# Newton-Schulz on X and its transpose: a second product in place of a turn, and a X inside the polynomial

## The reference

```
X = G / (sqrt(sum(G * G)) + 1e-7)          # G: 64 x 64, for 3 weights x 4 heads
for a, b, c in NS_COEFFS:                  # 5 sets of coefficients
    A = X @ X.T
    B = b * A + c * (A @ A)
    X = a * X + B @ X
```

## Time and profile before

| what | value |
|---|---|
| median of 3 runs (lowest to highest) | 861.67 us (861.62 to 861.74) |
| span of the profiled execution | 860.0 us, 27595 instructions |
| what lies around the span, against the median | 1.67 us |
| busy: PE, PEld | 811.3 us (94%), 700.2 us (81%) |
| busy: DVE, ACT, POOL | 715.6 (83%), 369.5 (43%), 406.7 us (47%) |
| transposes of X at line 701 | 450 matmuls, 64.2 us busy |
| each of the three kinds of small product | 1800 matmuls, 68.6 to 72.7 us busy |

### The profile page before, as it was taken

The page is one execution under the profiler, slowest core; times in us unless marked ns, Lnnn a source line. Parts: engine busy times, 40 slices in busy tenths (PEclk is TensorE's granted clock), DMA queues, the critical chain, the costliest instruction groups (busy, mean ns, idle before and its releaser), DMA issues.

```text
span 860.0 us, 27595 instructions
## 1 busy us (share of the span) xinstructions
PE 811.3 (94%) x9926; PEld 700.2 (81%) x9926; DVE 715.6 (83%) x2592; ACT 369.5 (43%) x868; POOL 406.7 (47%) x535
## 2 busy tenths in 40 slices
PE   3899999999999999999999999999999999999997
PEld 2888888888888788888888888888888888888886
DVE  4789798897988979889798897988979889798876
ACT  2444344443444434444444444444444444444433
POOL 1644545445454454544545445544455444544442
PEclk9899999999999999999999999999999999999999
DMA  8100000000000000000000000000000000000000
GB/s 326 35 3 14 8 2 19 0 12 6 0 18 0 12 6 0 18 0 12 6 0 18 0 12 6 0 18 0 12 6 0 18 0 12 6 0 12 0 12 7
DMA packets 9716, 13.77 MB, mean 16 GB/s; under 512 B 1120, under 2 KB 8928, under 8 KB 9440
## 3 DMA queue, kind: packets, MB, share of 16 engines
q1 hardware_dynamic: 7904, 7.80, 3.1%
q10 hardware_dynamic: 1792, 5.70, 1.7%
HBM read 11.41 MB, written 2.10 MB: 16 GB/s over the span
## 4 chain that ended last, share of the span: by engine, by line
PE 62%; DVE 26%; issue 7%; ACT 2%; POOL 1%; DMA 1%; DVEq 1%; SPq 0%; ACTq 0%
PE CB L630 13%; PE M L630 13%; PE YB L630 11%; PE HB L630 9%; PE CA L630 7%; DVE acc L1322 5%; PE CA L701 5%; DVE Wn L1169 4%; DVE X L1140 2%; DVE dhb L1089 2%; POOL r L286 1%; DVE Am L1126 1%; DVE Mp L1132 1%; DMA rows<-in_rows 1%; DVE r L1233 1%
## 5 line engine op out<-in xcount | busy, mean ns | idle before, releaser
L364 POOL TENSOR_TENSOR hq<-hr 128x512 f32<-128x512 f32 x128 | 136.3, 1065 | 77.7 <-ACT hr L427 76.2
L286 POOL TENSOR_TENSOR r<-r,half 128x3 f32<-128x3 f32 (+1 forms) x78 | 77.9, 1011 | 157.6 <-DVE r L1111 68.6
L630 PE MATMUL HB<-xlT,e_s 128*128 128x128 f32 x1024 | 144.0, 284 | 0.4 <-ACT xlT L427 0.4
L630 PE MATMUL YB<-e_s,hq 128*128 128x128 f32 x1024 | 141.6, 281 | 0.8 <-DVE acc L1322 0.8
L342 POOL TENSOR_TENSOR aX<-X,a_tile 128x192 f32<-128x192 f32 x150 | 92.9, 639 | 88.9 <-DVE X L1140 88.9
L630 PEld LDWEIGHTS HB<-xlT,e_s 128*128 128x128 f32 x1024 | 126.9, 193 | 7.7 <-ACT xlT L427 0.7
L427 ACT ACTIVATE hr<-HB 128x512 f32<-128x512 f32 x128 | 76.4, 597 | 130.0 <-PE HB L630 129.9
L1322 DVE SCALAR_TENSOR_TENSOR acc<-YB,cw,acc 128x128 f32<-128x128 f32 x448 | 125.5, 343 | 7.6 <-PE YB L630 7.6
L630 PEld LDWEIGHTS YB<-e_s,hq 128*128 128x128 f32 x1024 | 124.2, 192 | 5.6 <-issue 1.3
L427 ACT ACTIVATE XT<-CA 64x384 f32<-64x384 f32 x150 | 65.7, 477 | 63.3 <-PE CA L701 63.2
L630 PEld LDWEIGHTS CA<-Am 64*64 64x64 f32 x1800 | 60.8, 134 | 21.3 <-issue 15.9
(11 more groups left out here) (178 smaller groups left out, 1458.5 us busy)
## 6 DMA issues: line engine op xcount, KB each, us to landing
xa<-in_x SPq DMA_DIRECT2D x16, 128.0 KB, 2.0
e_s<-in_e1T ACTq DMA_DIRECT2D x1, 2048.0 KB, 12.7
e_s<-in_e2T ACTq DMA_DIRECT2D x1, 2048.0 KB, 19.0
xr<-in_x SPq DMA_DIRECT2D x16, 128.0 KB, 2.1
out<-ot SPq DMA_DIRECT2D x16, 128.0 KB, 1.7
wall<-in_wall SPq DMA_DIRECT2D x1, 820.0 KB, 6.8
up_s<-in_upT ACTq DMA_DIRECT2D x1, 512.0 KB, 14.1
down_s<-in_downT ACTq DMA_DIRECT2D x1, 512.0 KB, 19.6
```

The costliest lines, as they stand in the source:

```text
L286: return pool.tensor_tensor(dst, src, expo[:, 0:n], ALU.pow)
L364: pool.tensor_tensor(hq[b][:, :, :], hr[b][:, :, :], hr[b][:, :, :], ALU.mult).then_inc(e_hq, 1)
L630: return pe.matmul(out_, lhsT, rhs, start=start, stop=stop)
```

## The change

The transpose of X is no longer turned after each iteration. A second set of six products makes X_new^T = X^T Mp, where Mp now holds the term a X: A becomes A + (a/b) I before it enters the polynomial, so that c Mp X is the whole new X. GpSimd makes the shifted A (`AmI`) after VectorE's copy of A, in place of `aX` after X. Stage 3 of an iteration issues, for each group, the products for the transpose into `CA` and then those for X into `CB` (only the latter in the last iteration). ScalarE's copy of the transpose takes c as its scale and is now 128 partitions x 192 elements; the first iteration still turns X and copies it in two halves. The gram product goes into `CA`, and the square into `CB`.

```diff
-            def ax(i, g, it):
-                pool.wait_ge(e_x[g], (NI + 1) * i + it + 1)
-                pool.tensor_tensor(aX[g], X[g], a_tile[:, it, :], ALU.mult).then_inc(e_ax[g], 1)
+            def a_shift(i, g, it):
+                pool.wait_ge(e_am[g], NI * i + it + 1)
+                pool.tensor_tensor(AmI[g], Am[g], shift[:, it], ALU.add).then_inc(e_shifted[g], 1)
...
-                    if st % 4 == 0:
+                    if st % 4 == 1:
                         for g in range(G):
-                            ax(i, g, st // 4)
+                            a_shift(i, g, st // 4)
...
             def xt(i, g, it):
                 act.wait_ge(e_t[g], NI * i + it + 1)
-                a(XT[g], CA[g][0:HD, 0:3 * P], ACT.Copy).then_inc(e_xt[g], 1)
+                if it == 0:
+                    for h in range(2):
+                        c = slice(h * HD, (h + 1) * HD)
+                        ins = a(XT[g][c, :, :], CA[g][0:HD, 0:3 * P].rearrange("p (w c) -> p w c", w=3)[:, :, c], ACT.Copy)
+                    ins.then_inc(e_xt[g], 1)
+                else:
+                    a(XT[g], CA[g][:, 0:3 * HD], ACT.Copy, scale=NS[it - 1][2]).then_inc(e_xt[g], 1)
...
+            def ns_square(g, it):
+                am_in[g].wait()
+                if it > 0:
+                    x_in[g].wait(skip=1 if it == NI - 1 else 0)
+                ns_pair(g, CB, Am, Am).then_inc(e_prod[g], 1)
+
+            def ns_apply(g, it):
+                mp_in[g].wait()
+                if it < NI - 1:
+                    ns_pair(g, CA, X, Mp).then_inc(e_t[g], 1)
+                ns_pair(g, CB, Mp, X).then_inc(e_prod[g], 1)
...
             def ns_m(i, g, it):
                 dve.wait_ge(e_prod[g], 3 * NI * i + 3 * it + 2)
-                scalar_tensor_tensor(Mp[g], Am[g], b / c, CA[g], ALU.mult, ALU.add).then_inc(e_mp[g], 1)
+                dve.wait_ge(e_shifted[g], NI * i + it + 1)
+                scalar_tensor_tensor(Mp[g], AmI[g], b / c, CB[g], ALU.mult, ALU.add).then_inc(e_mp[g], 1)
             def ns_x(i, g, it):
                 dve.wait_ge(e_prod[g], 3 * NI * i + 3 * it + 3)
-                dve.wait_ge(e_ax[g], NI * i + it + 1)
-                scalar_tensor_tensor(X[g], CB[g], NS[it][2], aX[g], ALU.mult, ALU.add).then_inc(e_x[g], 1)
+                tensor_scalar(X[g], CB[g], NS[it][2], None, ALU.mult).then_inc(e_x[g], 1)
...
-            for it in range(NI):
-                nc.vector.memset(a_tile[:, it, :], NS[it][0])
...
+            dve.wait_ge(e_ident, 16)
+            tensor_tensor(eye, ident[:, 0:HD], ident[:, HD:P], ALU.add).then_inc(e_eye, 1)
+            dve.wait_ge(e_eye, 1)
+            for it in range(NI):
+                tensor_scalar(shift[:, it], eye (broadcast over w), NS[it][0] / NS[it][1], None, ALU.mult)
```

More of the change, by code:

```diff
@@ L105, in build @@
         neghalf = sb("neghalf", [P, 8])
-        a_tile = sb("a_tile", [P, NI, 3 * HD])
+        eye = sb("eye", [P, HD])
+        shift = sb("shift", [P, NI, 3, HD])
         bdones, mask, mask_prev = fixed[:, 0, :], fixed[:, 1:3, :], fixed[:, 3, :]
@@ L118, in build @@
         X = [sb(f"X{g}", [P, 3, HD]) for g in range(G)]
-        aX = [sb(f"aX{g}", [P, 3, HD]) for g in range(G)]
-        XT = [sb(f"XT{g}", [HD, 3, P]) for g in range(G)]
+        AmI = [sb(f"AmI{g}", [P, 3, HD]) for g in range(G)]
+        XT = [sb(f"XT{g}", [P, 3, HD]) for g in range(G)]
         Am = [sb(f"Am{g}", [P, 3, HD]) for g in range(G)]
@@ L222, in build @@
         e_dw, e_G, e_s3, e_ssb, e_sst, e_pw, e_x = (per_group(n) for n in ("dw", "G", "s3", "ssb", "sst", "pw", "X"))
-        e_ax, e_t, e_xt, e_am = (per_group(n) for n in ("aX", "turn", "XT", "Am"))
+        e_shifted, e_t, e_xt, e_am = (per_group(n) for n in ("AmI", "turn", "XT", "Am"))
         e_prod, e_mp = (per_group(n) for n in ("product", "Mp"))
@@ L229, in build @@
         e_ap, e_prT, e_av, e_at2, e_comb, e_ct, e_combT = (sem(n) for n in ("probs_turned", "prT", "att_pv", "att_steps", "comb", "comb_turned", "combT"))
-        e_mask = sem("mask_ready")
+        e_mask, e_eye = sem("mask_ready"), sem("eye")
         e_rt, e_cw = sem("route_steps"), sem("cw_ready")
@@ L338, in ss_pow @@
                 power(r3[g][:, 2, :], r3[g][:, 1, :], half, 3).then_inc(e_pw[g], 1)
-            def ax(i, g, it):
-                pool.wait_ge(e_x[g], (NI + 1) * i + it + 1)
-                pool.tensor_tensor(aX[g][:, :, :].rearrange("p w c -> p (w c)"),
-                                   X[g][:, :, :].rearrange("p w c -> p (w c)"), a_tile[:, it, :],
-                                   ALU.mult).then_inc(e_ax[g], 1)
+            def a_shift(i, g, it):
+                pool.wait_ge(e_am[g], NI * i + it + 1)
+                pool.tensor_tensor(AmI[g][:, :, :].rearrange("p w c -> p (w c)"),
+                                   Am[g][:, :, :].rearrange("p w c -> p (w c)"),
+                                   shift[:, it].rearrange("p w c -> p (w c)"), ALU.add).then_inc(e_shifted[g], 1)
             def row_pow(m, g):
@@ L478, in xt @@
                 act.wait_ge(e_t[g], NI * i + it + 1)
-                a(XT[g][:, :, :].rearrange("p w c -> p (w c)"), CA[g][0:HD, 0:3 * P], ACT.Copy).then_inc(e_xt[g], 1)
+                if it == 0:
[4 more added lines that the diff above has]
+                else:
+                    a(XT[g][:, :, :].rearrange("p w c -> p (w c)"), CA[g][:, 0:3 * HD], ACT.Copy, scale=NS[it - 1][2])\
+                        .then_inc(e_xt[g], 1)
             def w_T(m, g):
@@ L618, in _ @@
         def _(pe):
-            x_turn = [Expect(pe, e_x[g], f"x_turn{g}") for g in range(G)]
+            x_in = [Expect(pe, e_x[g], f"x_in{g}") for g in range(G)]
             xt_in = [Expect(pe, e_xt[g], f"xt_in{g}") for g in range(G)]
@@ L696, in sums, with ns_turn @@
                 mm(CB[g][:, 0:3], bdones[:, :], r3[g][:, 0, :]).then_inc(e_ssb[g], 1)
-            def ns_turn(g, last_step):
-                x_turn[g].wait(skip=1 if last_step else 0)
+            def ns_turn(g):
+                x_in[g].wait()
                 for w in range(3):
@@ L702, in ns_turn, with ns_pair @@
                 ins.then_inc(e_t[g], 1)
[L704 to L714, removed]
+            def ns_pair(g, bank_, left, right):
                 for w in range(3):
@@ L718, in ns_pair, with ns_gram @@
                         ins = mm(bank_[g][c, w * HD:(w + 1) * HD], left[g][c, w, :], right[g][c, w, :])
-                ins.then_inc(e_prod[g], 1)
+                return ins
+            def ns_gram(g):
+                xt_in[g].wait()
+                ns_pair(g, CA, XT, XT).then_inc(e_prod[g], 1)
+            def ns_square(g, it):
[8 more added lines that the diff above has]
+                ns_pair(g, CB, Mp, X).then_inc(e_prod[g], 1)
             def turn_w(m, g):
@@ L917, in body @@
                         if st % 4 == 0:
-                            ns_turn(g, st // 4 == NI - 1)
+                            if st == 0:
+                                ns_turn(g)
                             if st == 0 and g == 0:
@@ L925, in body @@
                         elif st % 4 == 2:
-                            ns_pair(g, CA, am_in, Am, Am)
+                            ns_square(g, st // 4)
                         else:
-                            ns_pair(g, CB, mp_in, Mp, X)
+                            ns_apply(g, st // 4)
                     for f in fill.get(st, []):
@@ L1125, in ns_a @@
                 dve.wait_ge(e_prod[g], 3 * NI * i + 3 * it + 1)
-                nc.vector.tensor_copy(Am[g][:, :, :].rearrange("p w c -> p (w c)"), CB[g][:, 0:3 * HD]).then_inc(e_am[g], 1)
+                nc.vector.tensor_copy(Am[g][:, :, :].rearrange("p w c -> p (w c)"), CA[g][:, 0:3 * HD]).then_inc(e_am[g], 1)
             def ns_m(i, g, it):
@@ L1138, in ns_x @@
                 dve.wait_ge(e_prod[g], 3 * NI * i + 3 * it + 3)
-                dve.wait_ge(e_ax[g], NI * i + it + 1)
-                nc.vector.scalar_tensor_tensor(X[g][:, :, :].rearrange("p w c -> p (w c)"), CB[g][:, 0:3 * HD], NS[it][2],
-                                               aX[g][:, :, :].rearrange("p w c -> p (w c)"), ALU.mult, ALU.add)\
-                    .then_inc(e_x[g], 1)
+                nc.vector.tensor_scalar(X[g][:, :, :].rearrange("p w c -> p (w c)"), CB[g][:, 0:3 * HD], NS[it][2], None,
+                                        ALU.mult).then_inc(e_x[g], 1)
             def row_sums(m):
@@ L1389, in _ @@
             ln_norm(0)
+            dve.wait_ge(e_ident, 16)
+            nc.vector.tensor_tensor(eye[:, :], ident[:, 0:HD], ident[:, HD:P], ALU.add).then_inc(e_eye, 1)
+            dve.wait_ge(e_eye, 1)
+            for it in range(NI):
+                nc.vector.tensor_scalar(shift[:, it], eye[:, :].unsqueeze(1).to_broadcast([P, 3, HD]),
+                                        NS[it][0] / NS[it][1], None, ALU.mult)
             dve.wait_ge(e_ttw, 16 * G)
```

2 lines of the change are left out of this document (1 added, 1 removed).

## The result

| kernel | median us (lowest to highest, runs) | against the kernel before, 95% interval |
|---|---|---|
| before | 861.7 (861.62 to 862.52, 4) | |
| changed | 895.02 (894.17 to 895.43, 4) | 1.0387 (1.0372 to 1.0401), slower |

The changed kernel's profiled execution has a span of 893.6 us and took 895.43. Over 15 tiles the 33.3 us are 2.2 us a tile. The prediction was 895.5 us. Two of its terms were far off, in opposite directions, so the agreement of the total is in part luck; the experiments show the true parts.

What follows compares the result with a forecast made beforehand. The prediction took a full TensorE queue to bound the Newton-Schulz phase, with one link on VectorE. It summed 1.6 + 0.65 = 2.25 us a tile, x 15 = 33.8 us, to 895.5 us (range 889 to 901).

Steps and rivals of the forecast that it cites:

- What bounds the kernel: Newton-Schulz phase is a full TensorE queue, not a latency chain; one link, X to Mp in iterations 2 to 3, is VectorE's.
- Part 1, TensorE's queue: Iterations 0 to 3: 24 added matmuls at 0.84 us replace turns at 0.65; net 0.76 us a tile, 11.4 us.
- lower bound of part 3: Up to Mp of iteration 3: 0.9 us, since X of the second group waits for all 48 products even without n8.
- Part 2, the copies: ScalarE's late XT copies stall TensorE 0.2 us at stage 7 to 8 and 0.5 us at stage 15 to 16.
- Part 3, the shift: Stage 9: n8 queues behind GpSimd's shifts, VectorE waits; Mp of iteration 3 is 1.55 to 1.6 us later.
- The walk: Before-and-after times at stage 9: ss8 ends 431.55 instead of 430.52, n8 434.8 instead of 432.23, qkn 435.95 instead of 434.30.
- Part 4, the last iteration: Stage 17: gram late by 0.5 us, the shifts add 0.15 before Mp; 0.65 us, bounds 0.4 and 1.1.
- Mp released by GpSimd at stage 17: Sign expected in the changed profile: at stage 17 Mp is released by GpSimd.
- TensorE's sum alone: Rival: VectorE's and GpSimd's lateness is swallowed by waits; 11.4 us or less plus one copy stall, 873 us, chance 0.14.
- More lock: Rival: the shifts also hold up routing steps and the token normalisation, +0.6 us a tile, 905 us; chance 0.12.
- n8 does no harm: Rival: 0.9 us up to Mp of iteration 3 plus the end's 0.65, 1.55 x 15 = 23, 885 us; chance 0.22.
- The faster rival: The chain decides, not the queue: 0.48 us a tile gained, 854.5 us, if TensorE's idle time exceeds 0.76 us; chance 0.04.

Runs made afterwards that it cites:

- e11: e3 with the products for the transpose left out too (TensorE's 1440 added matmuls gone): 832.9 us, ratio 0.9653.
- e3: Changed kernel without the shifted A, and XT copies moved ahead of h_relu(5) (for stage 8) and the table load (for stage 16): 866.41 us, ratio 1.0048.
- e2: Changed kernel without GpSimd's shifted A; Mp made from A itself, the term a X left out: 879.84 us, ratio 1.021.
- e5: Complete changed kernel with XT copies ahead of h_relu(5) (for stage 8) and the table load (for stage 16): 883.99 us, ratio 1.0243.
- e9: Complete changed kernel with one wait added on GpSimd: h_sq(5) starts only when VectorE has finished qkn: 879.32 us, ratio 1.0194.
- e4: Changed kernel with the power in prep_n8 replaced by a multiplication, nothing moved: 880.11 us, ratio 1.0198.
- e6: Changed kernel with GpSimd's power n8 ahead of the two shifts of stage 9 instead of behind them: 894.35 us, ratio 1.0369.
- e1: Kernel before with the shifted A in place of aX, the turns of X kept: 880.34 us, ratio 1.0213.

## Why the prediction came out, point by point

**What bounds the kernel: right.** Until iteration 2 the tile is a full TensorE queue: e11 loses 0.7 us for each stage of 24 products taken away, and in e3 VectorE's ss8 stands at +0.04.

**Part 1, TensorE's queue: sized wrong.** The step "24 matmuls ... cost what a like stage costs, 0.84 us" took the price of a stage with its start-up. In the earlier trace rows the 0.84 hold about 0.14 for leaving the wide shape (0.49 for the first 12 against 0.35 for the others); products added to a stage that is already running don't pay that again. They cost 0.70, and the turn 0.65. For the first swap the net is the 0.05 that this gives, by the starts of TensorE's gram products in the tile (11.78 and 11.82 us in iteration 0 for the kernel before and e3, 19.27 and 19.35 in iteration 1). The second costs 0.23 (26.85 and 27.16), for a reason that no run looks into, and the third 0.05 again (33.89 and 34.25). That makes 0.33, while three iterations came to 0.57 in my sum. My lower bound, 0.78, was too high as well. The first 12 against the next could be read in the old chain, had I split it by group. About 0.25 us a tile do follow from the products in another way, which the prediction had only as a lower bound of part 3: X comes behind 48 of them, and VectorE waits.

**Part 2, the copies: right at stage 15 to 16, another path at 7 to 8.** Stage 15 to 16: 0.5 predicted, 0.56 in the waits. Stage 7 to 8: a stall of TensorE of 0.2 predicted, and there is none; its gram products start at 27.16 us of the tile with the late copies and with the early ones (e3). The late copy works through VectorE instead: ss8 is 0.48 late, of which 0.08 were there before, and Am of both groups stands behind it. With both places, 0.9 us a tile (e2 less e3, 13.4 us, the hold of qkn in e2 among them) against 0.7. With the shift in place they are worth 11.0 us (e5). The table load took 1.28 us with the copy 0.02 behind it, as before, so the drain of the Trainium skill's page (ScalarE: Activation LUTs, What ACT_TABLE_LOAD costs) isn't seen here either: what the load costs is its place in the list.

**Part 3, the shift: place right, mechanism half right, sized wrong.** Two errors ran against each other. The walk had the step behind n8 about 1.6 us late (434.8 against 433.18); it is 0.92 late (31.58 against 30.66 us of the tile). Most of the difference is that of ss8, 1.03 late in the walk and 0.48 in the trace: 48 products take 1.54 us and not 1.68, and ScalarE's steps, which I had added end to end to 1.47 us from HB's end to the second copy, overlap and take 1.18 (444.27 to 445.45). Against it, the prediction took the chain behind n8 as 1.12 us, as before, and it came to 2.52 (449.80 to 451.07 + 1.25). h_sq(5) had run ahead of these steps (432.19 to 433.23 us before), and h_sq(6) behind them and `aX`; now both run right when the steps do and take the port twice. The wait for n8 itself is worth little, at most 0.14 at the second X (e9). e4 and e6 can't say this: in e4 qkn is held without the wait, and in e6 another wait takes its place. The Trainium skill (SBUF — State Buffer, Who interferes with whom) has it that, of a GpSimd and a VectorE operation that both need the shared port pair, the later one blocks until the other is done, and the rows bear it out: `gs`, with two SBUF inputs, ends at 436.81 and GpSimd's square at 436.79, and the tensor_scalar of eight elements ends at 450.80 and its square at 450.77. I had named the rule for stages 5 and 17 and for `gs`, and not for the very steps whose delay I was computing. I even credited the squares' earlier slot at `gs` with 0.25 us; it gives 0.5 (e1: +1.88 to +1.31).

**Part 4, the last iteration: the first half right, the second nil.** The gram's 0.5 us is there; the extra 0.15 us of the shift at stage 17 isn't: e2 and e4, without and with the shift, are at +1.21 and +1.22 at the second Mp of iteration 4. Mp released by GpSimd at stage 17 was one of the signs that I had named, and it isn't in the trace: VectorE's waits there are for TensorE.

**The sum.** Predicted: 1.6 up to Mp of iteration 3 and 0.65 behind it. Measured: 1.76 and 0.53 (at the second Mp of iteration 4), less 0.1 in the tail. But the 1.6 were composed of 0.57 for products, 0.2 for the copy and 0.8 for n8; as differences of runs at that Mp they are about 0.25 for products (e3), 0.4 for the copy (e2 less e3) and 1.1 for the port (the changed kernel less e9). The overcharge of the products, the step behind n8 put too late, and the missing hold of the port cancelled, and that is luck.

**The rivals.** TensorE's sum alone, at 873, is refuted in its size (e3: 866) and as the cause. "More lock" had the kind of cause right and the steps wrong: the lock costs 1.1 us a tile, at r and qkn, while the token normalisation takes 1084 ns against 1085 before. Other terms were smaller than forecast, so the total isn't 905. "n8 does no harm" is what e4 shows, but by 880 and not 885. The faster rival needed more than 0.76 us of idle time; the net charge turned out as 0.05 to 0.23 an iteration, so it was nearer than its chance said: with every order repaired the changed kernel is still 0.56% (0.40 to 0.71) slower.

**Left open.** The 0.3 us a tile that e3 keeps are seen on VectorE's wait for X; making the products for X before those for the transpose would test this. It wasn't run. Why the second swap costs TensorE 0.23 us and the others 0.05 is open too.

## What to carry to other kernels

When engines work through lists written by hand, the price of an edit is mostly in who stands behind the moved instruction: here 27 of 33 us were places in ScalarE's and GpSimd's lists and went away without touching the arithmetic. When a wait is taken off or delayed on VectorE, look also at what GpSimd will be doing at the new time, since a tiny step can be held for a whole GpSimd operation; a wait added on the engine that is ahead can be a gain. And price work added to a running stage by its second group, not by a stage that pays the start.

## What I had not expected of the hardware

- One added wait on GpSimd made the kernel 15.7 us faster (e9). The square had started 0.07 us before an 8-element step of VectorE, which then took 1.00 us instead of 0.16.
- Small products cost 0.35 us for 12 behind other small products and 0.49 behind wide ones. The 0.35 holds with one bank written for each group (a stage of 24 in 0.84) and with two (48 in 1.54).
- The gram product with its two halves on different partitions (71.8 us busy for 1800) is no faster than with both on the same 64 (72.2).
